# Four transformer layers on one core: query pieces on VectorE, gates loaded a body ahead, and other steps at other places

## What is computed

```python
shift1, scale1, gate1, shift2, scale2, gate2 = split(silu(c) @ ada_w + ada_b, 6)
x = x + gate1 * attention(norm(x) * (1 + scale1) + shift1)      # 16 heads of 9 features
x = x + gate2 * (gelu(h2 @ fc1_w + fc1_b) @ fc2_w + fc2_b)      # h2: the second norm, modulated; 576 hidden
# layer 1: norms are rms norms, and q and k are normed for each head as well
# layers 2, 3: layer norms, attention over the 128 tokens of a sequence
# layer 4: attention is over the heads of one token
attn = softmax(einsum('nthd,ntkd->nthk', q * scale, k)); out = einsum('nthk,ntkd->nthd', attn, v)
```

## Time and profile before

| | |
|---|---|
| median of three runs | 1532.93 us |
| the profiled execution's own time | 1541.48 us |
| its span | 1539.7 us |
| TensorE matmul busy | 1294.8 us (84%) |
| TensorE weight load busy | 834.6 us (54%) |
| VectorE busy | 1100.0 us (71%) |
| ScalarE busy | 964.1 us (63%) |
| GpSimd busy | 324.2 us (21%) |
| chain that ended last | PE 48%, ACT 17%, DVE 11%, issue 11%, DMA 5% |
| mean granted clock of TensorE | 0.926 |

### The profile page before, as it was taken

How to read it: one execution, slowest core, us unless ns; L and a number is a source line. 1 busy time by engine, 2 the same in 40 slices (tenths; PEclk the granted TensorE clock), 3 DMA queues, 4 the chain that set the end, 5 groups by cost and what they waited for, 6 DMA issues and landing times.

```text
span 1539.7 us, 36822 instructions
## 1 busy us (share of the span) xinstructions
PE 1294.8 (84%) x13282; PEld 834.6 (54%) x13314; DVE 1100.0 (71%) x2807; ACT 964.1 (63%) x2139; POOL 324.2 (21%) x446
## 2 busy tenths in 40 slices
PE   6375779889879999999999999999688788888886
PEld 4122345555546666666666666666465556565654
DVE  3755667777768888888888888888466666765542
ACT  0032556666647767777767777777567676877663
POOL 2010111211121112122112121122322332323201
PEclk9975978999979999999999999999789989989898
DMA  6313344423455544444444444555997899969800
GB/s 182 92 31 87 93 111 111 110 63 72 118 133 126 133 119 124 122 118 119 118 119 118 119 119 119 129 129 127 110 70 123 115 92 108 97 135 128 65 25 23
DMA packets 198482, 163.63 MB, mean 106 GB/s; under 512 B 80137, under 2 KB 182481, under 8 KB 192161
## 3 DMA queue, kind: packets, MB, share of 16 engines
q1 hardware_dynamic: 189920, 153.60, 52.7%
q10 hardware_dynamic: 8384, 7.69, 1.7%
HBM read 98.05 MB, written 62.41 MB: 104 GB/s over the span
## 4 chain that ended last, share of the span: by engine, by line
PE 48%; ACT 17%; DVE 11%; issue 11%; DMA 5%; SPq 3%; ACTq 3%; another core or an unknown queue 0%; POOL 0%; DVEq 0%; POOLq 0%
PE lin L1513 11%; PE lin L1497 9%; PE o_bank L1450 5%; ACT p_room L729 4%; PE score_bank L1344 4%; ACT hT_last L710 3%; DVE maxima L1120 3%; PE st_bank L1419 3%; PE score_bank L1388 3%; ACT h2T L715 2%; DMA gates<-gates_dram 2%; PE lin L1501 2%; ACT stack_room L800 2%; PE score_bank L1354 2%; ACT h1T L715 1%
## 5 line engine op out<-in xcount | busy, mean ns | idle before, releaser
L1120 DVE TENSOR_REDUCE maxima<-score_bank 128x4 f32<-128x512 f32 x512 | 329.2, 684 | 143.6 <-PE score_bank L1388 141.2
L729 ACT ACTIVATE p_room<-st_bank 128x512 f32<-128x512 f32 x512 | 278.4, 604 | 143.1 <-PE st_bank L1419 96.7
L1513 PE MATMUL lin<-w_f,gelu 128*128 128x144 f32 (+1 forms) x1280 | 199.8, 319 | 23.5 <-ACT max_T L812 22.9
L1513 PEld LDWEIGHTS lin<-w_f,gelu 128*128 128x128 f32 (+1 forms) x1280 | 187.8, 217 | 32.2 <-ACT max_T L812 30.4
L613 POOL TENSOR_TENSOR part_low<-qk_rest,part_mid 96x512 bf16<-96x512 f32 x96 | 113.9, 1187 | 416.8 <-DVE part_mid L1103 416.8
L1497 PE MATMUL lin<-h2T,w_h 128*128 128x512 f32 (+1 forms) x320 | 174.1, 644 | 4.5 <-ACT h2T L715 2.7
L1388 PE MATMUL score_bank<-stack_room 62*128 62x128 bf16 x2048 | 106.4, 226 | 84.8 <-ACT stack_room L800 38.4
L1450 PE MATMUL o_bank<-p_room,v_room 128*32 128x128 f32 x4096 | 171.9, 288 | 0.0
L604 POOL TENSOR_TENSOR x<-x,gated 128x288 f32<-128x288 f32 x64 | 53.9, 842 | 461.2 <-DVE gated L1168 461.2
L1388 PEld LDWEIGHTS score_bank<-stack_room 62*128 62x128 bf16 x2048 | 61.4, 97 | 158.9 <-issue 48.1
L845 ACT ACTIVATE gelu<-lin 128x512 f32<-128x512 f32 (+1 forms) x160 | 91.2, 589 | 84.6 <-PE lin L1501 71.6
(11 more groups left out here) (193 smaller groups left out, 2395.1 us busy)
## 6 DMA issues: line engine op xcount, KB each, us to landing
stack_room<-stack_dram SPq DMA_DIRECT2D x96, 512.0 KB, 8.2
stack_dram<-part_high SPq DMA_DIRECT2D x64, 288.0 KB, 4.0
gates<-gates_dram SPq DMA_DIRECT2D x64, 288.0 KB, 3.9
norm_room<-stack_dram SPq DMA_DIRECT2D x32, 512.0 KB, 8.5
stack_dram<-part_mid SPq DMA_DIRECT2D x64, 192.0 KB, 2.7
stack_dram<-part_high SPq DMA_DIRECT2D x64, 144.0 KB, 3.9
stack_dram<-part_mid SPq DMA_DIRECT2D x64, 96.0 KB, 3.0
stack_dram<-part_low SPq DMA_DIRECT2D x64, 96.0 KB, 2.3
```

Source lines behind the costliest of these rows:

```text
L729: eng.activation(probs[:, i % PBUFS, :], st_bank[i % 2][:, :], ACT.Exp, scale=float(HD) ** -0.5)\
L1120: eng.tensor_reduce(maxima[:, b, CH * c:CH * c + CH], bank_of(f"S{i}")[:, :].rearrange("p (h k) -> p h k", h=CH), AX_X, ALU.max)\
L1513: ins = eng.matmul(o, gelu[0:k, T, b * TOK:(b + 1) * TOK], w_f2[l][0:k, T, :], start=T == 0, stop=T == FCT - 1)
```

## The change

ScalarE's `order_queries` keeps pieces 4 to 7 of layer four; VectorE gets pieces 0 to 3, after the second `mid` and after the first normalisation of M. There are two semaphores for the queries instead of one. `load_gates(g - 2, 1)` in body g becomes `load_gates(g - 1, 1)`, behind the load of the values and of the first maxima. In layer one the stores of the parts go behind the load of the second maxima, the three squares go behind the third gelu, `high` of tiles 0 and 1 behind the seventh pair of exponentials, the fits ahead of the second statistics, and the last `mid` into the next body, behind its first `raw`. `copy_max(J, 0)` and `flip_max(J, 0)` come earlier, `divide(P, 3)` ahead of `split_max(g, 2)`, and `divide(g, 2)` between the gating of the attention's output and its addition to x.

```diff
 # uses_of
-    order += ([] if late else scores[3]) + [("mT0", J), ("OD1", g)] + (scores[3] if late else [])
+    order += [("mT0", J)] + ([] if late else scores[3]) + [("OD1", g)] + (scores[3] if late else [])
 # SyncE, body
                 load_max(g, 2)
                 store_values(J)
-                load_gates(g - 2, 1)
                 if not normed_heads(L):
                     store_parts(L)
                 load_max(g, 3)
                 store_out(g - 3)
                 load_gates(g, 0)
                 load_values(J)
                 load_max(J, 0)
-                if normed_heads(L):
+                load_gates(g - 1, 1)
+                if normed_heads(L) and not normed_heads(g + 3):
                     store_parts(L)
                 load_max(J, 1)
+                if normed_heads(L) and normed_heads(g + 3):
+                    store_parts(L)
                 load_stack(L)
 # ScalarE, order_queries and body
-                if b == 0:
+                if b == 2:
                     need(eng, "st_done", g - 2, STEPS - 1)
...
-                if late:
-                    square(L, 0)
-                    square(L, 1)
...
                 gelus(Q, (0, 1))
+                copy_o(g, 0)
+                gelus(Q, (2,))
                 if late:
-                    square(L, 2)
-                copy_o(g, 0)
-                gelus(Q, (2, 3, 4))
+                    for T in range(QKT):
+                        square(L, T)
+                gelus(Q, (3, 4))
...
-                order_queries(J, 0)
                 exponentials(g, 3)
...
                 modulated(M, 0, 0)
-                order_queries(J, 1)

                 exponentials(g, 5)
                 modulated(M, 0, 1)
                 if flow_is(J, "a"):
                     values(J, 0)
+                order_queries(J, 2)
+
+                copy_max(J, 0)
+                exponentials(g, 6)
                 if late:
                     high(L, 0)
                     high(L, 1)
-                order_queries(J, 2)
-
-                exponentials(g, 6)
-                copy_max(J, 0)
                 copy_oT(g, 1)
 # VectorE
+            def order_queries(g, b):
+
+                if not flow_is(g, "t"):
+                    return
+                need(eng, "stack_loaded", g, STACK_LOADS - 1)
+                if b == 0:
+                    need(eng, "st_done", g - 2, STEPS - 1)
+                for k in (2 * b, 2 * b + 1):
+                    eng.tensor_copy(*piece_of(g, 0, k)).then_inc(S["ordered_q"], 1)
...
+            def add_attention(g, h):
+
+                if not ok(g):
+                    return
+                need(eng, "proj_gated", g, h)
+                eng.tensor_tensor(pair_of(g, h), pair_of(g, h), gated[0][:, h, :], ALU.add).then_inc(S["x_attn"], 1)
...
                 if ok(L):
                     mid_or_raw(L, 1)
+                if normed_heads(J) and late:
+                    mid(J, 2)
                 maxima_of(g, 5)
+                divide(P, 3)
                 split_max(g, 2)
-                divide(P, 3)
...
                     mid_or_raw(L, 2)
+                order_queries(J, 0)
                 maxima_of(g, 6)
...
                 residual(P, 1, 0)
+                add_attention(P, 1)
                 maxima_of(J, 0)
                 divide(g, 0)
                 normalise(M, 0)
+                order_queries(J, 1)
...
                 if late:
-                    statistics(P, 1)
                     fit(L, 0)
                     fit(L, 1)
+                    statistics(P, 1)
...
                 residual(g, 0, 0)
                 divide(g, 2)
+                add_attention(g, 0)
                 maxima_of(J, 4)
                 if late and normed_heads(M):
                     mid(L, 1)
-                    mid(L, 2)
 # TensorE
-                    need(eng, "ordered_q", g, pair + 1)
+                    need(eng, "ordered_q" if pair < 4 else "ordered_q_late", g, pair % 4 + 1)
...
                 shifted_scores(g, 6)
+                flip_max(J, 0)
                 if not late:
                     scores(J, 3)
                 weighted_values(g, 5)
-                flip_max(J, 0)
                 flip_o(g, 1)
```

More of the change, by code:

```diff
@@ L167 @@
     "mods1": 2, "mods2": 2,
-    "v_mixed": 4, "ordered_q": PIECES, "ordered_k": PIECES,
+    "v_mixed": 4, "ordered_q": PIECES // 2, "ordered_q_late": PIECES // 2, "ordered_k": PIECES,
     "qk_rest": QKT, "qk_sq": QKT, "norm_done": 1, "norm_max": 1, "norm_ln": 1, "norm_exp": 1, "norm_y2": 1, "norm_t": 1,
@@ L177 @@
                  "v_stored": GB, "v_loaded": 1}
-TOKEN_ONLY = {"v_mixed", "ordered_q", "ordered_k", "v_stored", "v_loaded"}
+TOKEN_ONLY = {"v_mixed", "ordered_q", "ordered_q_late", "ordered_k", "v_stored", "v_loaded"}
 FIRST_TOKEN_GROUP = FLOW.index("t") * GROUPS
@@ L438, in load_stack @@
                     return
-                need(eng, "ordered_q", L - 1, PIECES - 1)
+                need(eng, "ordered_q", L - 1, PIECES // 2 - 1)
+                need(eng, "ordered_q_late", L - 1, PIECES // 2 - 1)
                 need(eng, "ordered_k", L - 1, PIECES - 1)
@@ L799, in order_queries @@
                     out_piece, in_piece = piece_of(g, 0, k)
-                    eng.activation(out_piece, in_piece, ACT.Copy).then_inc(S["ordered_q"], 1)
+                    eng.activation(out_piece, in_piece, ACT.Copy).then_inc(S["ordered_q_late"], 1)
             def copy_max(g, b):
@@ L1170, in residual @@
                    .then_inc(S[gated_name], 1)
-                if which == 1:
+            def add_attention(g, h):
+                if not ok(g):
                     return
-                need(eng, gated_name, g, h)
-                eng.tensor_tensor(pair_of(g, h), pair_of(g, h), gated[0][:, h, :], ALU.add).then_inc(S[x_name], 1)
+                need(eng, "proj_gated", g, h)
+                eng.tensor_tensor(pair_of(g, h), pair_of(g, h), gated[0][:, h, :], ALU.add).then_inc(S["x_attn"], 1)
             eng.wait_ge(setup["x"], 64)
```

## The result

| | before | changed |
|---|---|---|
| median, us | 1532.45 (4 runs, 1531.14 to 1533.51) | 1479.51 (4 runs, 1476.62 to 1485.1) |
| profiled execution, span, us | 1541.5, 1539.7 | 1485.1, 1483.4 |
| TensorE, VectorE, ScalarE busy, us | 1294.8, 1100.0, 964.1 | 1256.1, 1121.3, 935.5 |

What follows compares the result with a forecast made beforehand. TensorE was taken to bound layers two and three, with slack in waits and lowered clock in layers one and four. Terms of 11 + 21 + 26.5 + 14 + 9.5 = 82 us gave 1451 us, range 1415 to 1495.

Steps and rivals of the forecast that it cites:

- The first step: Layers two and three: division ahead of the residual's addition removes a 0.45 us wait and moves the next product 0.5 us.
- The step that failed: Layers two and three: early flip stands 0.9 us for h1T, yet the MLP product starts 0.15 us earlier instead of 0.56.
- The rival that was slower by the early flip: TensorE stands at the flip for ScalarE, 0.9 us in each of 17 bodies; 1548 us, chance 0.05.
- The five waits: Layer one, TensorE: raw copy 1.16, h2T 1.56, maxima's DMA 0.73, MLP product 1.30, fourth scores 0.81 us; reduced or gone.
- the 7.2 us taken to be free a body: Layer one: TensorE alone would gain about 5.5 us a body from waits and 1.7 from the clock.
- VectorE's term: Layer one: VectorE's work without a hole gives back 1.7 us a body; next projection and scores come only 1.8 earlier.
- The stack's: Layer one: TensorE meets the stack load about 2 us too soon, giving back 2.0 us a body.
- the floor: Layer four, full bodies: DMA engines, empty only 5.3 of 48.0 us, limit a body to 42.7 us.
- The term for the clock: Layer four, full body: mean clock 0.89 over 48 us means 5.3 us at half speed, 2.6 us lost.
- The 5.9 in body 23: Entry to layer four: clock of 0.80 over 58.5 us costs 5.9 us, part of 18 us of waits.
- rival "half": VectorE late from extra work and GpSimd locks, stack load the wait in both layers, clock falling: 1492 us, chance 0.20.
- the forecast case itself: Whole kernel: the summed terms give 82 us saved and 1451 us, spanning 1425 to 1475; chance 0.65.

Runs made afterwards that it cites:

- cheap pieces: The changed kernel with every layer-four piece copied without the change of order, so other values are computed; 1459.6 us, one run.
- the one it was made from: The changed kernel with the early flip put behind the fourth scores and ahead of the sixth weighted values; 1461.45 us (0.9562).
- the best kernel: That flip placement, plus layer four's first two key pieces copied on VectorE and GpSimd's other six held until then; 1456.75 us (0.9529).

## Why the prediction was right in layer four and wrong elsewhere

**Layers two and three: -0.9 us for -11.** The first step held: the division is worth 0.50. The step that failed is the next: TensorE "stands about 0.9 us there, which swallows a short wait before the next scores; I estimate that the product starts 0.15 earlier". The 0.99 us was there, but it swallowed only 0.29. What stands behind the flip in TensorE's order is not the product alone but the fourth scores, and on them hang VectorE's maxima and, at the end of the body, its subtraction. The term was not +0.15 but -0.42 (36.23 with the flip at its old place, 36.65 with the early one). The rival that was slower by the early flip had the mechanism, at half its price, and only together with a loss elsewhere that did not come.

**Layer one: -5.5 for -21.** The five waits went, as forecast. Of the 7.2 us taken to be free a body, 1.7 were the clock before the second half of the MLP product. That half did run at full clock (2.72 us, in bodies 2 to 4 of all eight profiles with the changed order), but the first half, now behind the wait for the stack, ran slower in 21 of these 24 bodies, for example 4.34 for 2.67: the loss moved, it did not go. VectorE's term was right (taken 1.7, measured 1.39 + 0.38 at the body's end). The stack's was too small: taken 2.0, measured 2.8 to 3.25. By these 7.2 - 1.7 - 3.1 - 1.8 is 0.6; at equal clock 0.2 and 0.5 were measured. Yet the layer as a whole gained more than that: it took 291.8 to 296.7 us in the four profiles with the old order and 282.2 to 290.8 in the eight with the new one, 7 us less on average. That the rest comes through the clock (0.86 to 0.88 before, 0.89 to 0.91 after) is likely; how the change raises it is not shown. Putting the subtraction back did not help: the body's load, VectorE and the load of the maxima each stand ready to be the last.

**Layer four: -50.5 for -50, by parts that missed.** That the sum fits is luck: bodies 24 to 28 gave 9 us too much and the others 8.5 too little. Full bodies gained 7.1 each where 5.3 were taken. Of the 1.8, 1.2 come from the body that was read: it took 48.0 us, the shortest of five, which took 49.2 on average (47.9 in the kernel with the division alone). The other 0.6 is the step that failed, the floor: "the DMA engines end it later", at 42.7; the five took 42.1. The share counts the time of packets, not a capacity. The changed kernel, mean of 16 engines:

```profile
1245.00:1248.00 3.00, 3.00 (x54) 2.35 (x53) 1.89 (x4) 2.94 (x9) 0.82 (x1) 1.00 1.25 187
1260.00:1263.00 3.00, 2.99 (x23) 1.79 (x21) 2.81 (x9) 2.04 (x4) 2.25 (x3) 1.00 1.93 15
```

A share of 1.93 moves 15 GB/s and one of 1.25 moves 187, so a share of 1.00 in the earlier trace rows did not say that the engines were full; bodies of 40.3 and, with cheap pieces, 38.4 us went below the floor. The term for the clock beside it was too small as well: "5.3 us at half speed, 2.6 us lost" halves twice, for a mean of 0.89 between full and half speed is 10.6 us at half speed and 5.3 lost. TensorE's busy time in body 27 fell by 3.7 (40.4 at 0.89, 36.7 at 1.00), and in the two layer-one bodies at 0.90 and 1.00 it differs by 4.4, where the forecast's way would give 2.5. The 5.9 in body 23 has the same error. Body 23 gave 6.7 for 14 in the first profile, but it took 54.3 in the kernel with the division alone, an edit worth 0.5 us a body, where the kernel before took 58.5, and 49.4 in the second profile of the changed kernel: a body read once carries some 4 us of its own. VectorE's piece, taken at 0.75 from bounds of 0.51 and 1.07, is 0.57 by itself, and 1.09 on average.

**The rule on the ports.** The pair of 5.20 us beside GpSimd's 3.99 is the row. "SBUF — State Buffer" (Who interferes with whom) of the Trainium skill calls it an exclusive lock. The trace agrees, and it works both ways: in body 26, where VectorE started first, its pair (first row) took 1.16 us and GpSimd's (second) 2.99.

```profile
1214.64 1.16 DVE L1161 COPY stack_room<-norm_room 128x512 bf16<-128x512 bf16 x2 [1.62 <-DMA norm_room<-stack_dram]
```

```profile
1214.70 2.99 POOL L627 COPY stack_room<-norm_room 128x512 bf16<-128x512 bf16 x2
```

On the lock the forecast's rival "half" rested, at 1492. The lock came, its price was small: TensorE has other work for most of a held pair, its waits behind them are 5.7 us in the changed kernel, and the kernel that keeps GpSimd away from VectorE's pieces is 4.7 us faster than the one it was made from (6.4 in bodies 24 to 30 of the profiles).

**The range** held the time because layer four came out whole, by luck in its parts, and because it took in the rival "half": 1479.5 lies outside the 1425 to 1475 of the forecast case itself, and is nearer to that rival (1492) than to 1451. The rival's reason holds in part: in layer one the stack load became TensorE's wait and the clock stayed below full; in layer four TensorE ran at 0.99 and only VectorE waited for the load, 13.9 us over the eight groups. Of the signs named, the repeated body shortened by 0.07 us where 0.65 was forecast, and VectorE's pieces went over 1.1 us, which was to be a sign of being wrong; they did so only beside GpSimd's.

## What to carry to other kernels

An instruction moved forward on an in-order engine is paid by whatever it is moved ahead of: list what hangs on those instructions on the other engines, and try the place in between; here it was worth 0.84 us in each of 17 bodies, more than either end. Where several waits end at nearly the same time (gates and pieces, stack and VectorE), undoing one shows little and the next stands there: cost the pair, not each. Read the clock beside every body before a difference of 3 us is given to an edit.

## What the runs showed of the hardware

- The same copy of 128 x 512 bf16, with the read elements 64 bytes apart and then contiguous: VectorE 571 and 282 ns, ScalarE 1067 and 629, GpSimd 1023 and 602. The order of reading costs 0.3 us on VectorE and 0.4 on the others; strided, VectorE is still the fastest by nearly half.
- A VectorE copy beside GpSimd's copies is held for their whole run, once for 4.7 us across four of them, and small casts with it: in the best kernel the cast of the maxima, 128 x 16, took 0.92 us while GpSimd copied, and 0.17 in a body of layers two and three of the kernel before.

```profile
1242.15 0.92 DVE L1134 CAST max_parts<-maxima 128x16 bf16<-128x16 f32 x1
```

```profile
1241.97 2.04 POOL L629 COPY stack_room<-norm_room 128x512 bf16<-128x512 bf16 x2
```

- The DMA share goes over 1 while the engines move little (1.93 at 15 GB/s).
- A wait for a DMA can be put down to "issue": the 2.72 us for gates above.
